# Part of the next step's queries and keys, and of the last factor product, made inside the nucleus steps

## The reference

```python
def _adj_from_feats(Xa, W1, W2, W3):
    Q = Xa @ W1                      # 256 -> 64
    K = Xa @ W3
    logits = Q @ W2 @ K.T / TAU
    idx = jnp.argsort(-logits, axis=1)
    ...                              # keep the smallest set with 0.9 of the mass
    return jax.nn.softmax(masked, axis=1)

for s in range(STEPS):               # STEPS = 2
    A = _adj_from_feats(Xa, W1, W2, W3)
    Xf = Rf @ Xf
    Xb = Rb @ Xb
    Xa = A @ Xa
    Z = Z + (Xf @ U1[s] + Xb @ U2[s] + Xa @ U3[s])
Y = X + Z
```

## Time and profile before

| | us |
|---|---|
| median of 3 runs | 3665.94 (3665.34 to 3668.64) |
| the profiled execution's own time | 3668.13 |
| its span, first to last instruction | 3666.1 |
| PE busy in the span | 2938.1 (80%) |
| DVE busy | 2347.9 (64%) |
| ACT busy | 1252.7 (34%) |
| mean granted clock of TensorE | 0.931 |

### The profile page before, as it was taken

The page is one execution under the profiler, slowest core; times in us unless marked ns, Lnnn a source line. Parts: engine busy times, 40 slices in busy tenths (PEclk is TensorE's granted clock), DMA queues, the critical chain, the costliest instruction groups (busy, mean ns, idle before and its releaser), DMA issues. The chain is left out here.

```text
span 3666.1 us, 57967 instructions
## 1 busy us (share of the span) xinstructions
PE 2938.1 (80%) x20312; PEld 2140.7 (58%) x20312; DVE 2347.9 (64%) x4563; ACT 1252.7 (34%) x1676; POOL 50.0 (1%) x69
## 2 busy tenths in 40 slices
PE   1449999999999999999998566884774677775499
PEld 1236676766667676676765254663453465664388
DVE  7975555555565555556564698889588969684330
ACT  3433434344334443443433223332214434311211
POOL 0000000000000000000000100000000000000110
PEclk9989999999999999999999788997887888997699
DMA  5764848567483866838486110110010010100400
GB/s 190 292 235 117 201 99 199 126 172 189 110 197 97 200 144 152 202 95 197 106 190 163 40 58 12 58 47 1 21 35 24 12 35 12 35 24 21 194 1 24
DMA packets 585578, 396.80 MB, mean 108 GB/s; under 512 B 538339, under 2 KB 550630, under 8 KB 559846
## 3 DMA queue, kind: packets, MB, share of 16 engines
q1 hardware_dynamic: 583430, 380.47, 38.8%
q10 hardware_dynamic: 2016, 14.68, 1.0%
HBM read 223.06 MB, written 37.81 MB: 71 GB/s over the span
## 5 line engine op out<-in xcount | busy, mean ns | idle before, releaser
L667 DVE SCALAR_TENSOR_TENSOR e_lo<-e,e_hi 128x2048 f16<-128x2048 f32 x128 | 293.3, 2291 | 456.9 <-ACT e_hi L595 456.9
L549 PE MATMUL av<-vw_hi,pT_hi 128*128 128x256 f16 x2048 | 559.6, 273 | 7.5 <-DMA pT_lo<-e_lo 7.5
L549 PE MATMUL av<-vw_lo,pT_hi 128*128 128x256 f16 x2048 | 559.6, 273 | 0.0
L549 PE MATMUL av<-vw_hi,pT_lo 128*128 128x256 f16 x2048 | 559.6, 273 | 0.0
L538 PE MATMUL logits<-kT_hi,qT_hi 128*128 128x512 f16 x1024 | 389.1, 380 | 7.2 <-DVE att_small L653 5.5
L1741 DVE SCALAR_TENSOR_TENSOR nuc_junk<-nuc_e,nuc_thr 128x2048 bf16<-128x2048 f32 x168 | 388.4, 2349 | 5.1 <-issue 0.4
L538 PE MATMUL logits<-kT_hi,qT_lo 128*128 128x512 f16 x1024 | 388.2, 379 | 0.0
L538 PE MATMUL logits<-kT_lo,qT_hi 128*128 128x512 f16 x1024 | 388.2, 379 | 0.0
L589 ACT ACTIVATE att_small<-att_small,minus 128x1 f32<-128x1 f32 x128 | 37.7, 294 | 828.8 <-DVE att_small L662 828.8
L590 ACT ACTIVATE e<-e,att_small,sc 128x2048 f32<-128x2048 f32 x128 | 266.1, 2079 | 0.0
L595 ACT ACTIVATE e_hi<-e 128x2048 f16<-128x2048 f32 x128 | 244.6, 1911 | 15.3
(11 more groups left out here) (397 smaller groups left out, 5883.8 us busy)
## 6 DMA issues: line engine op xcount, KB each, us to landing
bias<-bias_scratch SPq DMA_DIRECT2D x130, 1028.0 KB, 4.8
bias_scratch<-adj_bias SPq DMA_DIRECT2D x16, 1028.0 KB, 3.9
adjT_scratch<-adjT SPq DMA_DIRECT2D x16, 1024.0 KB, 7.0
nuc_at_hi<-adjT_scratch SPq DMA_DIRECT2D x32, 512.0 KB, 3.9
nuc_at_lo<-adjT_scratch SPq DMA_DIRECT2D x32, 512.0 KB, 4.8
adjT<-adjT_scratch SPq DMA_DIRECT2D x16, 1024.0 KB, 21.0
adj_rows<-in_adj_dram ACTq DMA_DIRECT2D x14, 1024.0 KB, 8.5
hx<-in_x_dram SPq DMA_DIRECT2D x1, 2048.0 KB, 8.5
```

Source lines behind the costliest of these rows:

```text
L549: last = nc.tensor.matmul(AV[par][:, :], PT[par][w][:, m, :], VW[x][:, m, :], start=(m == 0 and w == x == 0), stop=(m == T - 1 and w == 1))
L667: nc.vector.scalar_tensor_tensor(out=EL[:, :], in0=E[par][:, :], scalar=P_SCALE, in1=EH[:, :], op0=ALU.mult, op1=ALU.subtract).then_inc(lo ...
```

## The change

Inside `nucleus` PE and ACT get a function `after(n)`. In step 0 it takes two finished tiles of `acc` (2n and 2n+1), turns them, multiplies by W1 and W3, then the queries by W2, and writes `QT` and `KT` of the next step. In step 1 it takes one tile, turns it, multiplies by `U3[1]`, adds `y` by a product with the identity and writes `y`. The table `AFTER` says where: in step 0 pairs 0 to 3 (tiles 0 to 7) after the second stretch of diffusion, pairs 4 and 5 (tiles 8 to 11) after the third; in step 1 tiles 0 to 3, 4 to 7 and 8 to 11 after the three stretches, tiles 12 to 15 within and behind `last_tiles`. The refresh `qk1` then turns and multiplies only the last quad (`first=3`), and cuts all four as before. The phase `u3` is gone, and `U3[1]` is a fourth weight tile loaded at the start of `nuc1`.

```diff
                     phase(refresh, f"qk{step}", acc if step == 0 else XA, X_, ident, halfp, norm=(step == 0),
-                          logits=(w1, w2, w3, QT, KT), parts=Xp, rows=X_SCALE)
+                          logits=(w1, w2, w3, QT, KT), parts=Xp, rows=X_SCALE, first=3 * step)
...
-                phase(refresh, "u3", XA, XA, ident, halfp, weight=a["L1_gnn_U3"][1], onto=Y)
...
-                    for b in range(QUADS):
+                    for b in range(first, QUADS):
                         turned(b)
-                        if b:
+                        if b > first:
                             products(b - 1)
...
+                if first:
+                    turned_copies(first)
                 for b in range(QUADS + 2):
...
                 for b in range(QUADS):
-                    if turn:
+                    if turn and b >= first:
                         read(b)
                     if parts and b:
                         cut(b - 1)
...
-        FACTORS = len(weights)
-        U = sb(c, name + "_u", [P, FACTORS, KC, D])
+        FACTORS = (2, 3)[step]
+        U = sb(c, name + "_u", [P, len(weights), KC, D])
...
+        cT = xT if step == 0 else sb(c, name + "_afterT", [P, D])
+        AFTER = (((), range(0, 4), range(4, 6)), (range(0, 4), range(4, 8), range(8, 12)))[step]
...
+                    if k == 0 and g:
+                        pe.wait_ge(c_done, sum(len(AFTER[n]) for n in range(g)))
...
+                def after(n):
+
+                    tiles = (2 * n, 2 * n + 1) if step == 0 else (n,)
+                    pe.wait_ge(out_s, tiles[-1] + 1)
+                    if n:
+                        pe.wait_ge(c_done, n)
+                    for k in range(KC):
+                        for m, t in enumerate(tiles):
+                            o = (k * len(tiles) + m) * P
+                            last = nc.tensor.transpose(TP[0][:, o:o + P], out[:, t, k * P:(k + 1) * P], ident[:, :])
+                    last.then_inc(c_tp, 1)
+                    pe.wait_ge(c_xt, n + 1)
+                    if step:
+                        for k in range(KC):
+                            nc.tensor.matmul(TP[1][:, 0:D], cT[:, k * P:(k + 1) * P], U[:, 3, k, :], start=(k == 0), stop=False)
+                        nc.tensor.matmul(TP[1][:, 0:D], ident[:, :], y[:, n, :], start=False, stop=True).then_inc(c_prod, 1)
+                        return
+                    for o, w in ((TP[1][0:64, 0:D], w1[:, :, :]), (TP[1][:, D:2 * D], w3x)):
+                        for k in range(KC):
+                            last = nc.tensor.matmul(o, w[:, k, :], cT[:, k * D:(k + 1) * D], start=(k == 0), stop=(k == 1))
+                    last.then_inc(c_prod, 1)
+                    pe.wait_ge(c_read, 2 * n + 1)
+                    nc.tensor.matmul(TP[0][:, 0:D], w2x, QT[0:64, n * D:(n + 1) * D], start=True, stop=True).then_inc(c_prod, 1)
...
                             if k + 1 < G:
                                 turn(k + 1, q)
+                        if step and k:
+                            after(i - 1)
+                    if step:
+                        after(T - 1)
...
                 for t in range(DIFFUSED[0], DIFFUSED[1]):
                     diffuse_tile(t)
+                for n in AFTER[0]:
+                    after(n)
                 logits(3, 0)
...
+                def after(n):
+                    s.wait_ge(c_tp, n + 1)
+                    if step:
+                        nc.scalar.activation(cT[:, :], TP[0][:, 0:D], ACT.Copy).then_inc(c_xt, 1)
+                        s.wait_ge(c_prod, n + 1)
+                        nc.scalar.activation(y[:, n, :], TP[1][:, 0:D], ACT.Copy).then_inc(c_done, 1)
+                        return
...
                 if step:
                     sums(2, 1)
+                for n in AFTER[0]:
+                    after(n)
                 for k in range(G):
                     halves(1, k)
```

More of the change, by code:

```diff
@@ L1204, in refresh @@
 def refresh(nc, sb, ps, sem, name, src, dst, ident, halfp, norm=False, weight=None, onto=None, logits=None,
-            parts=None, rows=None, bias=None, lo_gain=None):
+            parts=None, rows=None, bias=None, lo_gain=None, first=0):
     (stats_done, rstd_done, dve, centred, ready, tp_s, xt_s, prod_s, u_read, q_s, q_read, w_loaded, scaled, biased, w2_s, w2_read) = (
@@ L1261, in products @@
                     def products(b):
-                        pe.wait_ge(xt_s, KC * (b + 1))
+                        pe.wait_ge(xt_s, KC * (b - first + 1))
                         x = xT[b % 2]
@@ L1286, in _ @@
                     if logits is not None:
-                        pe.wait_ge(q_read, 2 * QUADS)
-                        for b in range(QUADS):
+                        pe.wait_ge(q_read, 2 * (QUADS - first))
+                        for b in range(first, QUADS):
                             nc.tensor.matmul(TP[b // 2][b % 2][:, :], w2x, QT[0:64, b * BANK:(b + 1) * BANK],
@@ L1293, in _, with turned_copies @@
             def _(s):
+                def turned_copies(b):
+                    s.wait_ge(tp_s, b - first + 1)
+                    if b >= first + 2:
+                        s.wait_ge(prod_s, b - first - 1)
+                    for k in range(KC):
+                        nc.scalar.activation(xT[b % 2][:, k, :], TP[b % 2][k][:, :], ACT.Copy).then_inc(xt_s, 1)
+                if first:
+                    turned_copies(first)
                 for b in range(QUADS + 2):
@@ L1298, in _ @@
                             nc.scalar.activation(dst[:, t, :], dst[:, t, :], ACT.Relu).then_inc(ready, 1)
-                    if turn and 1 <= b <= QUADS:
-                        s.wait_ge(tp_s, b)
-                        if b >= 3:
-                            s.wait_ge(prod_s, b - 2)
-                        for k in range(KC):
-                            nc.scalar.activation(xT[(b - 1) % 2][:, k, :], TP[(b - 1) % 2][k][:, :], ACT.Copy).then_inc(xt_s, 1)
+                    if turn and not first and 1 <= b <= QUADS:
+                        turned_copies(b - 1)
                     if parts and b >= 2:
@@ L1318, in read @@
                 def read(b):
-                    v.wait_ge(prod_s, b + 1)
+                    v.wait_ge(prod_s, b - first + 1)
                     if weight is not None:
@@ L1363, in _, with nucleus @@
                 if logits is not None:
-                    for b in range(QUADS):
-                        v.wait_ge(w2_s, b + 1)
+                    for b in range(first, QUADS):
+                        v.wait_ge(w2_s, b - first + 1)
                         nc.vector.tensor_copy(QT[:, b * BANK:(b + 1) * BANK], TP[b // 2][b % 2][:, :]).then_inc(w2_read, 1)
-def nucleus(nc, sb, ps, sem, name, QT, KT, parts, out, ident, diffusion):
+def nucleus(nc, sb, ps, sem, name, QT, KT, parts, out, ident, diffusion, next_logits):
     weights, at_d, scales, ident16, y, sc, Xp, Xf, Xb, step = diffusion
@@ L1385, in nucleus @@
     (aimed, summed) = (sem(f"{name}_{s}") for s in ("aimed", "summed"))
+    (c_tp, c_xt, c_prod, c_read, c_done) = (sem(f"{name}_{s}") for s in ("after_tp", "after_xT", "after_product", "after_read", "after"))
+    w1, w2, w3 = next_logits
+    w2x, w3x = w2[:, :, :].rearrange("p a n -> p (a n)"), w3[:, :, :, :].rearrange("p k a n -> p k (a n)")
     C = CUTS[step]
@@ L1474, in diffuse_tile @@
                     if t == 0:
-                        pe.wait_ge(u_loaded, 16 * FACTORS)
+                        pe.wait_ge(u_loaded, 16 * len(weights))
                     for r in range(FACTORS):
@@ L1594, in _ @@
                     diffuse_tile(t)
+                for n in AFTER[1]:
+                    after(n)
                 for k in range(G):
@@ L1598, in _ @@
                     diffuse_tile(t)
+                for n in AFTER[2]:
+                    after(n)
                 last_tiles()
@@ L1707, in _ @@
                     product(3, k)
+                    if step and k:
+                        after(LAST + k - 1)
+                if step:
+                    after(T - 1)
             @block.gpsimd
```

20 lines of the change are left out of this document (14 added, 6 removed).

## The result

The changed kernel takes 3640.83 us (median of 4 runs, 3639.12 to 3643.72) against 3666.72 us for the kernel before in the same session: a ratio of 0.9927 with a 95% interval of 0.9913 to 0.9942, so 25.9 us less. A repetition beside later experiments gave 0.9932 (0.9918 to 0.9945). The forecast was 29.3 us less. The traces of the change and of its repetition show how far a trace can be trusted: over the two steps together they agree to 0.3 us, but single places in them lie up to 1.8 us apart.

A forecast was written before the change was run, and what follows sets the result against it. Both refresh stretches were taken as serial and uncovered, while `nucleus` has PE holes, most of them waits for DVE. Terms -16.9 + 0.8 + 0 + 5.3 + 0 + 10.8 - 29.3 = -29.3 us gave 3637 us, range 3629 to 3649.

The forecast's parts named there:

- Part 1: Refresh between the steps: only tiles 12 to 15 turned, 16.9 us gained, 0.8 us taken back for slower first logits.
- Part 2: Six pairs added in step 0: hidden in PE's waits for DVE, cost 0 until a pair takes over 8.4 us.
- Part 3: Tiles 0 to 3 in step 1, behind ACT's sums: on the path, 5.3 us later, bounds 2.4 and 13.
- Part 4: Tiles 4 to 11 in step 1: hidden, 23 us of work against 31.8 us of waits, cost 0.
- Part 5: Tiles 12 to 15 in the last group of step 1: on the path, 10.8 us added, bounds 8 and 16.
- Part 6: Last refresh after step 1 removed: 29.3 us gained; its weight load, moved to step 1's start, costs 0.
- The rule that was weighed: PE's clock gate does not count transposes as activity, so chains a fifth transposes and a third idle likelier stay slow.
- Rival (a): Chains stay slow: tiles 0 to 3 cost 13 us, the last group some 4 more; 3649 us, chance 0.12.
- Rival (b): The chain of tiles 0 to 3 in step 1 is all warm: 2.4 for 5.3, 3634 us, chance 0.12.
- Rival (c): PE-ACT hand-overs cost far more: zero gain near 5.95 us a tile, about 3675 us at 6.5; chance 0.03.
- Rival (d): After the removed last refresh, the next phase waits for something; half that gain lost, 3652 us, chance 0.03.

The follow-up runs named there:

- step-0 half: The changed kernel with no last factor products inside step 1 and the separate phase `u3` back: 3649.4 us, 0.9952 of the kernel before.
- step-1 half: The changed kernel without the query and key pairs in step 0, the whole refresh between the steps as before: 3657.9 us, 0.9975 of the kernel before.
- chain of twelve tiles: The changed kernel with last-group products cut in two and tiles 0 to 11 all in step 1's third stretch: 3630.0 us, 0.9898 of the kernel before.

## Why the prediction held, and by how much it missed

The sign, the size and the range (3629 to 3649) held: 3640.8 us for 3637. By its steps, in traces:

- **Part 1**, the shorter refresh: 16.95 us forecast as 16.9, and shown alone by the step-0 half. The 0.8 us that I took back for a slower first logit group did not come: the group took 9.36 us after 3.83 us of idleness, 9.44 before.
- **Part 2**, the pairs: hidden. The four of the first hole took 25.5 us of it, 6.4 each, since the clock fell after the first (products of 2.14, then 3.58, 3.38 and 3.79 us); the two of the second took 4.8 each. I had 4.9 warm and 8.1 slow, and a threshold of 8.4, which the 6.4 stay under. The run with all six in one hole shows that it was the cover that made them free.
- **Part 3**, tiles 0 to 3 on the path: this is the step that was mis-sized. Forecast 5.3, measured 7.2 (12.2 of shift left of 19.4). I had put two tiles at the low clock and two at the high one; three were slow and one fast, and a slow one takes 4.63 us, not 4.3 (the terms that I had named for it add up to 4.2; what was short is the three matmuls, 2.93 us for my 2.63, and the hand-overs). The mechanism stands as forecast, and the run that keeps PE busy shows the clock in it; the waits of the four maxima were 4.09, 1.16, 1.16 and 1.15 us where I had named 2 to 3 and about 1.
- **Part 4**, tiles 4 to 11: hidden, with 15.65 us of wait left. But 2.6 us of shift were lost between the fourth maximum and the last group (12.2 to 9.6), for which I had no term. Some 1.5 are tile 12 of the diffusion, whose six matmuls took 4.54 us at a granted clock of 0.73 over its stretch, where the same tile took 2.86 before. Such slow tiles are in the kernel before too, at other places, and the repetition of the change had none here (its wait for the second sums is 16.73 us for 18.56). The remaining 1.1 stand behind DVE's wait ahead of the lists, 7.37 us for 5.64 in the kernel before. It is 5.62 in the step-1 half and 7.09 in the step-0 half, so it came with the half that changes nothing at this place (rows below); what it is in that half isn't shown. In the repetition the whole of this loss is 0.9 us.
- **Part 5**, tiles 12 to 15: 11.3 for 10.8 us. From PE's first product to the end of the last copy it is 3355.94 - 3315.86 = 40.1 us, against 3354.24 - 3325.43 = 28.8. The order is the one given: 1.11 us of wait for each of two copies, and two tiles in series at the end.
- **Part 6**, the last refresh: 29.15 us for 29.3. From that last copy to `onward` there are 0.98 us where there were 30.13. Its weight load, moved to the start of step 1, cost nothing that shows.

DVE's timeline, the rows that part 4 speaks of: the kernel before, and the step-1 half.

```profile
3285.39 0.88 DVE L1910 TENSOR_SCALAR nuc_listed<-nuc_eight,nuc_small 128x8 f32<-128x8 f32 x4 [5.64 <-issue]
...
3291.53 0.87 DVE L1980 TENSOR_SCALAR nuc_listed<-nuc_eight,nuc_small 128x8 f32<-128x8 f32 x4 [5.62 <-issue]
```

In the profiled executions the sum misses by 3.0 us (26.3 for 29.3). Missed were 1.9 in part 3, 2.6 in part 4, 0.5 in part 5, 0.15 in part 6 and 1.1 behind `onward`'s start, 6.3 in all; against them stand 2.0 ahead of step 0, which the change doesn't touch, and 1.3 in step 0 and part 1. That these cancel half of what was missed is luck. The 1.1 behind `onward`'s start are not the change's: the phases from there to the end take 281.7 us before, and 280.0 to 283.7 in the other programs, whose code there is the same.

**The rule that was weighed.** In the run with PE kept busy, and in the chain of twelve tiles, the granted clock stays 1.00 over 11 and 36 us of a chain that is a fifth transposes and a third idle, and the matmul groups stay at 1.13 us; so it does over the six pairs in one hole (29 us). The slow chain of part 3 rose by itself to 1.13 us at its fourth tile. The Trainium skill, "TensorE: Matmul & The Clock Gate", on transposes, has them not counted as activity; none of these chains was held down by its transposes. But a chain can lose the clock on its way. In the first hole of step 0 it fell after the first pair in the change, and in each of the other nine runs with four pairs there at least one pair was slow. This chain stands behind a diffused tile that is slow too (its products took 2.9 to 3.2 us, where the two tiles ahead of it took 1.99), in the kernel before as well. Whether the transposes have a part in that, no run shows, and it cost nothing only because the hole covered it.

Rival (a), chains that stay slow throughout, is refuted, by the tiles at 1.13 us. Rival (b), all warm, is refuted by the three slow tiles. Rival (c) needed tiles of nearly 6 us; they took 3.01 and 4.63. Rival (d) is refuted by the 0.98 us that are left where the phase stood.

## What to carry to other kernels

Work moved into a hole is free as far as that hole's wait reaches, and not where the wait is for the same engine that the work needs: the hole behind ACT's sums looked as long as the others and was the only one that cost. Look up the granted clock of the place where moved work will run: here 4.7 of the 7.2 us that the exposed chain cost were its clock, and behind the last diffused tile of step 1 it was the high one for nothing. It isn't a promise: the four pairs in the first hole of step 0 lost it on the way, at 6.4 us a pair for 5.18. And when a step moves in time, ask which transfers move with it: a 1 MB load that came to lie over DVE's jumps took back 2.2 of 7.3 us.

## What the runs showed of the hardware

- DVE's wait at a place where it jumps over four loops was 5.6 us in two runs and 7.1 to 7.5 us in nine with the DMA engines free of data, but for its first 0.7 us in one, and 9.6 to 9.7 us in the two in which 1 MB moved at 176 GB/s. In all of them it ends as the third of three instruction packets lands, 2.3 to 2.6 us behind one another; the first came after 0.8, 2.3 to 2.6, and 4.8 us. That the transfer held the first one back is read from this order; one pair of runs moved the transfer and nothing else of DVE's.
- A chain of PE and ACT that began at a clock of 0.50 had one to three tiles at 2.07 us before the first at 1.13; one that began at 1.00 had all twelve at 1.13. The chain of four pairs in step 0 began at 0.99 (2470 to 2476) and fell: it is 0.72 over its 24 us, while six such pairs in the other hole kept 1.00 over 29 us.
- The first products of the last group ran at 0.56 and 0.60 behind waits of 5.83 and 15.65 us, at 0.72 behind 3.41, and at 1.00 behind 1.63 us, which was worth some 1.9 us.
- The granted clock falls in the middle of dense work as well: one diffused tile of the change has 0.73 over 6 us, and its matmuls take 4.54 for 2.86 us. The tile differs from one program to the next.
